# Moving the sweeps over the 8-bit weights, and their maximum over partitions, to earlier places of a fused transformer kernel

## What is computed

```
x = x + tanh(g_xattn[0]) * L0_xattn(layernorm(x), ctx, mask, mask, Wq, bq, Wk, bk, Wv, bv)   # 16 heads
x = x + tanh(g_ffn[0])   * L0_ffn(layernorm(x), w_gate, w_up, w_down)
x = x + tanh(g_xattn[1]) * L1_xattn(layernorm(x), k, fside, ctx, ctx, 8)                    # long convolution
x = x + tanh(g_ffn[1])   * L1_ffn(layernorm(x), w_fc, w_proj)

L0_ffn:  gate = sigmoid(bitlinear(x, w_gate)); up = bitlinear(x, w_up); bitlinear(gate * up, w_down)
         bitlinear: x per row rounded to 8 bits (scale max|x|/127), w rounded to {-1, 0, 1} * mean|w|
L1_ffn:  _fp8_matmul(relu(_fp8_matmul(x, w_fc))^2, w_proj)
         _fp8_matmul: w scaled by scale_w = max(max|w| / 448, 1e-6) and cast to e4m3; x likewise
```

## Time and profile before

| | |
|---|---|
| median of 3 runs | 1229.68 us (1228.73 to 1229.90) |
| profiled execution, its own time | 1229.71 us |
| its span in the trace | 1227.9 us |
| PE busy | 1065.7 us, 87% |
| DVE busy | 994.6 us, 81% |
| ACT busy | 702.7 us, 57% |
| GpSimd busy | 514.1 us, 42% |

### The profile page before, as it was taken

How to read it: one execution, slowest core, us unless ns; L and a number is a source line. 1 busy time by engine, 2 the same in 40 slices (tenths; PEclk the granted TensorE clock), 3 DMA queues, 4 the chain that set the end, 5 groups by cost and what they waited for, 6 DMA issues and landing times. The chain is left out here.

```text
span 1227.9 us, 13948 instructions
## 1 busy us (share of the span) xinstructions
PE 1065.7 (87%) x4729; PEld 420.3 (34%) x4802; DVE 994.6 (81%) x1522; ACT 702.7 (57%) x846; POOL 514.1 (42%) x403
## 2 busy tenths in 40 slices
PE   3889889999999999778999979999999996379686
PEld 2444212222222222134444444444444443134232
DVE  4368879999999997298999947887888887687897
ACT  2777768888888888846566760110000000885996
POOL 2666313543543553711010118888878880000111
PEclk9989889999999999999999998999999997599789
DMA  9899834644644642151111111212121110000011
GB/s 322 264 383 379 267 121 128 189 123 137 191 124 133 197 125 84 41 198 36 51 38 50 35 56 35 69 52 69 52 68 52 61 59 1 0 1 1 18 52 69
DMA packets 73703, 132.89 MB, mean 108 GB/s; under 512 B 18336, under 2 KB 37152, under 8 KB 73120
## 3 DMA queue, kind: packets, MB, share of 16 engines
q1 hardware_dynamic: 73632, 132.00, 32.9%
HBM read 107.58 MB, written 22.02 MB: 106 GB/s over the span
## 5 line engine op out<-in xcount | busy, mean ns | idle before, releaser
L921 DVE TENSOR_REDUCE mneg<-ps_m 128x1 f32<-128x512 f32 x512 | 326.3, 684 | 35.5 <-PE ps_m L833 31.9
L1527 PE MATMUL ps_y<-kv,toeplitz_sb 128*128 128x512 f32 x640 | 279.2, 595 | 8.4 <-POOL kv L1457 8.4
L773 ACT ACTIVATE probs<-ps_s 128x1024 f32<-128x1024 f32 x256 | 250.7, 1023 | 41.8 <-PE ps_s L866 41.8
L1527 PEld LDWEIGHTS ps_y<-kv,toeplitz_sb 128*128 128x128 f32 x640 | 120.9, 191 | 154.8 <-issue 154.8
L866 PE MATMUL ps_s<-qk_stack 128*128 128x512 bf16 x473 | 132.8, 387 | 26.9 <-ACT probs L773 17.5
L876 PE MATMUL ps_o<-probs,v_all 128*17 128x512 f32 x1024 | 135.6, 602 | 0.2 <-ACT probs L773 0.2
L1457 POOL TENSOR_TENSOR kv<-vT,ctxT_sb 128x2048 f32<-128x2048 f32 x32 | 118.9, 3717 | 35.4 <-PE ps_y L1527 28.5
L1112 PE MATMUL ps_g<-w,xT_f 128*128 128x512 bf16 x492 | 116.7, 382 | 13.4 <-DVE h_f L1294 8.5
L833 PE MATMUL ps_m<-qk_stack 64*128 64x512 bf16 x512 | 112.7, 394 | 14.3 <-DVE mneg L921 6.7
L1501 ACT ACTIVATE w_anchor<-w_f 128x512 f32<-128x512 f32 x32 | 20.0, 627 | 164.9 <-DMA w_f<-in_w 164.9
L1590 DVE TENSOR_TENSOR z<-ps_y,ctxT_sb 128x1024 f32<-128x1024 f32 x64 | 77.7, 1217 | 43.3 <-PE ps_y L1527 43.3
(11 more groups left out here) (167 smaller groups left out, 1616.2 us busy)
## 6 DMA issues: line engine op xcount, KB each, us to landing
qk_stack<-qk_parts SPq DMA_DIRECT2D x192, 128.0 KB, 3.0
w_sweep<-in_w SPq DMA_DIRECT2D x8, 1536.0 KB, 12.0
qk_parts<-qk_part SPq DMA_DIRECT2D x16, 768.0 KB, 9.1
w_sweep<-in_w SPq DMA_DIRECT2D x16, 768.0 KB, 5.4
w_sweep<-in_w SPq DMA_DIRECT2D x16, 512.0 KB, 3.7
toeplitz_sb<-in_toeplitz SPq DMA_DIRECT2D x32, 256.0 KB, 2.6
w_f<-in_w SPq DMA_DIRECT2D x32, 256.0 KB, 2.9
v_rows<-vp SPq DMA_DIRECT2D x8, 544.0 KB, 10.1
```

Source lines behind the costliest of these rows:

```text
L773: nc.scalar.activation(pr[:, k % 2, 2 * slot:2 * slot + 2, :], S[:, 2 * slot:2 * slot + 2, :], ACT.Exp).then_inc(exp_done, 1)
L921: nc.vector.tensor_reduce(mneg[:, h, tc, hd:hd + 1], M[:, bank_, :], AX.X, ALU.max, negate=True).then_inc(max_red, 1)
L1527: mm = nc.tensor.matmul(Y[:, q % 3, l2, :], T[:, g % 2, (lt - m) * P:(lt - m + 1) * P], kv[:, g % 2, m, :], start=(m == 0), stop=(m == lt))
```

## The change

It moves work between stages and shifts buffers; no arithmetic is added or taken away.

- SP issues the first two loads of sweeps in attention's unit 15, when the scores of unit 14 are done, ahead of that unit's denominators; loads 2 and 3 stand ahead of the loads of ctxT. For this `w8c` moves to 28 to 36 KB, and `gate` of the convolution to where it fits.
- DVE prepares rows 0 and 1 and does sweeps 0 and 1 before tile 0. Tile t then does sweep t + 1, for t from 1 to 14: sweep 15 stands in tile 14, and tile 15 has none.
- `invert` of unit 15 moves from behind the third chunk of tile 0 to behind its first; the statistics of rows 14 and 15 move from tiles 0 and 1 to tiles 1 and 2; ln_vector and ln_scalar of these rows move from tile 2 to tile 4.
- GpSimd's maximum over partitions moves to behind update(12).
- DVE's first write to `z` in the convolution waits until the last take_down is done, as the new layout needs.

```diff
@@ attention, sync
             if last:
+                load_sweeps(sp)
                 gather_den(u, h, b)
@@ feed-forward, sync
+    def load_sweep(sp, i):
+        if i >= 2:
+            sp.wait_ge(w8m_ready, i - 1)
+        sp.dma_start(w8c[:, i % 2], A["w8"][2 * i:2 * i + 2].rearrange("m p l -> p m l"))\
+            .then_inc(w8c_loaded[i % 2], 16)
+
+    def load_sweeps(sp):
+        sp.wait_ge(scores_done, 2 * STEPS * (ROWT - 1))
+        load_sweep(sp, 0)
+        load_sweep(sp, 1)
...
@@ feed-forward, scalar
-                if c == 2 and same(t, 2):
+                if c == 2 and t == 4:
                     ln_scalar(core, act, 2)
@@ feed-forward, vector
         def finish_attention(t):
-            if t == 0:
-                invert(dve, ROWT - 1, 1, B - 1)
+            if t == 1:
                 att_statistics(dve, ROWT - 2)
-            elif t == 1:
+            elif t == 2:
                 att_statistics(dve, ROWT - 1)
-            else:
+            elif t == 4:
                 ln_vector(core, dve, 2)
...
         prepare(0, 0, 0)
+        prepare(1, 1, 1)
+        sweep(0, 0)
+        sweep(1, 1)
...
-                if c == 0 and not last:
-                    if not first:
-                        dve.wait_ge(xt_done, t)
+                if c == 0 and first:
+                    invert(dve, ROWT - 1, 1, B - 1)
+                if c == 0 and not first and not last:
+                    dve.wait_ge(xt_done, t)
                     prepare(t + 1, 1 - par, t + 1)
-                if c == 2 and not first:
-                    sweep(t - 1, 1 - par)
+                if c == 2 and not first and not last:
+                    sweep(t + 1, 1 - par)
...
             if last:
                 quantise(t, par, t)
-                sweep(t, par)
                 statistics(dve, t - 1)
@@ feed-forward, gpsimd
         for t in range(ROWT - 1):
             update(pool, t)
+            if t == ROWT - 4:
+                largest_weight(pool)
@@ long convolution
-    def gpsimd(pool):
+    def largest_weight(pool):
         pool.wait_ge(w8_run, ROWT)
         nc.gpsimd.partition_all_reduce(w8s[:, MA, :], core.w8_max, P, bass.bass_isa.ReduceOp.max)\
             .then_inc(w8_all, 1)
+
+    def gpsimd(pool):
...
             weights(g)
+            if g == 0:
+                dve.wait_ge(d_taken, ROWT)
             weigh(g, 0)
```

More of the change, by code:

```diff
@@ L633, in load_next, with sync @@
             load_constants(core, sp, 1, 1)
-    def sync(sp):
+    def sync(sp, load_sweeps):
         def gather_den(u, h, b):
@@ L1030, in phase_bitlinear @@
     KB = 1024
-    xn, xq, xT, sg, h, hq, hT, ds, sc, w8m, w8c = overlay(
+    xn, xq, xT, sg, h, w8c, sc, w8m, hq, hT, ds = overlay(
         nc, "ffn", 0, ("xn_f", [P, 2, L], F32), ("xq_f", [P, 2, L], BF16), ("xT_f", [P, 2, LT, P], BF16),
-        ("sg_f", [P, 2, L], F32), ("h_f", [P, 2, FF], F32), ("hq_f", [P, 2, FF], BF16), ("hT_f", [P, 2, KT, P], BF16),
-        ("down_sums", [P, 1, L], F32), ("sc_f", [P, 2, 16], F32), ("w8_max_t", [P, 2, 2], F32),
-        ("w8_sweep1", [P, 2, 2, L], F32))
+        ("sg_f", [P, 2, L], F32), ("h_f", [P, 2, FF], F32), ("w8_sweep1", [P, 2, 2, L], F32),
+        ("sc_f", [P, 2, 16], F32), ("w8_max_t", [P, 2, 2], F32), ("hq_f", [P, 2, FF], BF16),
+        ("hT_f", [P, 2, KT, P], BF16), ("down_sums", [P, 1, L], F32))
     core.cT, = overlay(nc, "cT", 92 * KB, ("ctxT_sb", [P, LT, B, C], F32))
@@ L1052, in phase_bitlinear @@
     wd = core.w3[:, 2].rearrange("p a b -> p (a b)").rearrange("p (k o) -> p k o", k=KT)
-    def sync(sp):
[L1055 to L1063, removed]
+    def load_sweep(sp, i):
[7 more added lines that the diff above has]
+        load_sweep(sp, 1)
+    def sync(sp):
+        load_sweep(sp, 2)
+        load_sweep(sp, 3)
         sp.wait_ge(x_updated, ROWT)
@@ L1066, in sync @@
             sp.dma_start(core.cT[:, lt], A["ctxT"][lt * P:(lt + 1) * P]).then_inc(core.cT_loaded, 16)
-        for t in range(2, ROWT):
-            tile(t, t % 2, False, t == ROWT - 1)
+        for i in range(4, ROWT):
+            load_sweep(sp, i)
     def tensor(pe, turn_in):
@@ L1297, in tile @@
                     chunk_max(t, par, c - 1)
-                if c == 0 and not last:
-                    if not first:
-                        dve.wait_ge(xt_done, t)
+                if c == 0 and first:
+                    invert(dve, ROWT - 1, 1, B - 1)
+                if c == 0 and not first and not last:
+                    dve.wait_ge(xt_done, t)
                     prepare(t + 1, 1 - par, t + 1)
-                if c == 2 and not first:
-                    sweep(t - 1, 1 - par)
-                if c == 2 and t < 3:
+                if c == 2 and not first and not last:
+                    sweep(t + 1, 1 - par)
+                if c == 2:
                     finish_attention(t)
@@ L1330, in update, with gpsimd @@
         nc.gpsimd.tensor_tensor(xt, xt, ds[:], ALU.add).then_inc(xf_updated, 1)
-    def gpsimd(pool):
+    def gpsimd(pool, largest_weight):
         for t in range(ROWT - 1):
             update(pool, t)
+            if t == ROWT - 4:
+                largest_weight(pool)
     after = (shift_ready, xq_ready, hq_ready, h_ready, d_taken, xf_updated, w8_run, update, statistics)
-    return Phase(sync, gpsimd, scalar, tensor, vector), after
+    return Phase(sync, gpsimd, scalar, tensor, vector), load_sweeps, after
 def phase_longconv(core, ctx, A, before):
@@ L1629, in vector @@
         statistics(ROWT - 1)
-    return Phase(sync, gpsimd, scalar, tensor, vector), turn_in, normalise_ahead, place
+    return Phase(sync, gpsimd, scalar, tensor, vector), turn_in, normalise_ahead, place, largest_weight
 TWO20 = 2.0 ** 20
@@ L2007, in build @@
          vector_first) = first
-        bt, rest = phase_bitlinear(core, ctx, A, *tail)
-        cv, turn_in, normalise_ahead, place = phase_longconv(core, ctx, A, rest)
+        bt, load_sweeps, rest = phase_bitlinear(core, ctx, A, *tail)
+        cv, turn_in, normalise_ahead, place, largest_weight = phase_longconv(core, ctx, A, rest)
         with nc.Block() as block:
@@ L2014, in _ @@
                 pj.sync(sp, load_first, load_next)
-                at.sync(sp)
+                at.sync(sp, load_sweeps)
                 bt.sync(sp)
@@ L2022, in _ @@
                 at.gpsimd(pool)
-                bt.gpsimd(pool)
+                bt.gpsimd(pool, largest_weight)
                 cv.gpsimd(pool)
```

5 lines of the change are left out of this document (2 added, 3 removed).

## The result

| | before | after |
|---|---|---|
| median | 1229.79 us (4 executions, 1228.73 to 1232.18) | 1219.53 us (4, 1218.88 to 1221.34) |
| ratio after to before | | 0.9913, 95% interval 0.9899 to 0.9928 |
| profiled execution | 1229.71 us | 1219.38 us |
| its span | 1227.9 us | 1217.6 us |
| first convolution | 739.65 us | 731.52 us |

A second set of 6 executions gave 0.9927 (0.9911 to 0.9943). The change saves about 10 us, where 11.6 were forecast.

What follows compares the result with a forecast made beforehand. The convolution is PE-bound but waits 8.4 us for GpSimd's kv, held by two code switches. Seam 7.8, clock 1.7 and start 1.1 - 0.5 + 0.9 + 0.6 sum to 11.6: 1229.7 to 1218.1 us, range 1215.5 to 1222.5.

Steps and rivals of the forecast that it cites:

- The switches and the missing gap: End of feed-forward: GpSimd's two switches (5.57, 6.90 us) run before update(13), so kv runs inside down(15) and PE continues without gap.
- Clock 1.7: Start of the convolution: without PE's gap its clock does not fall, 1.7 us gained (bounds 0 and 1.8).
- Seam 7.8: End of feed-forward to first convolution: PE goes on at about 731.8 instead of 739.65, 7.8 us gained.
- now waits until 718.9, 0.9 later than before ... it slips by 0.5 us: End of feed-forward: DVE's row 13 statistics wait for late update(13), so round_h(15) and down(15) slip by 0.5 us.
- GpSimd comes back later than reckoned: Rival, end of feed-forward: update(14) goes before L1247, DVE and its chain wait 1.3 us; 1219.4 us, chance 0.13.
- +1.1 - 0.5 + 0.9 + 0.6 = 2.1: Start of feed-forward: 1.1 us from tile 0, 0.5 lost to roundings, 0.9 from tile 1, 0.6 net from tile 2.
- Tile 0 gave its term: Tile 0: PE's fourth chunk no longer waits for DVE's second product behind prepare(1), 1.1 us gained.
- the 0.6: Tile 2: with ln_vector moved and PE in time, less the statistics moving in, net 0.6 us gained (bounds 0.6 either way).
- The roundings' 0.5: Before tile 0: prepare(1) beside GpSimd's last three roundings makes PE start 0.5 us later (bounds 0.2 and 1.6).
- The term of 0.9 for tile 1: Tile 1: GpSimd's last normalise comes earlier and delays prepare(2) less, 0.9 us gained (bounds 0 and 1.9).
- ln moved: nothing: Tiles 2 and 4: ln_vector moves to tile 4 with all it costs, since DVE is as full there; nothing gained.
- roundings and DVE exclude each other: Rival, start of feed-forward: each rounding waits for a prepare(1) operation, PE starts 1.6 us later, not 0.5; 1219.2 us, chance 0.10.

## Why the prediction was right, and where its terms were not

The time was forecast as 1218.1 us and is 1219.5, inside the range, and the mechanism is the one forecast: GpSimd's switches held the first kv, and the maximum now runs them where the first kv does not wait. DVE does, and that was priced too low.

- **The switches and the missing gap: right.** all_reduce and both switches kept their lengths; kv waits for place 7; PE has no idle time before the convolution. The kernel with the maximum put back has the old time.
- **Clock 1.7: right.** The convolution's busy time went from 279.2 to 277.5 us, in every profile in which PE did not wait for kv.
- **Seam 7.8: mis-sized, measured 6.0, and 4.7 to 6.0 in the five profiles that end so.** The step "now waits until 718.9, 0.9 later than before ... it slips by 0.5 us" saw the wait and took it for the only price. round_h slipped by 1.6 us against tile 15 (14.78 us behind its start in before, 16.39 after): 1.05 for the later start of L1252, 0.95 for its meeting update(14), less 0.4 for which ACT itself had been busy. That meeting was my second rival, "GpSimd comes back later than reckoned", with a chance of 0.13; its 1219.4 us is nearer to what came out than the forecast. It is the rule here, not the exception: update(14) was on time, 14.0 us behind the start of tile 15, in all five profiles, and the late update(13) pushes quantise to just that place, so that one of L1250 to L1252 was drawn out in each (to 0.79 to 2.33 us). So round_h slipped by 1.1 us more than forecast. Another 0.9 us I had at nothing: PE's wait grew from 1.66 to 3.26 us, and the transposes and down(15) ran at the low clock. From round_h to the convolution it was 9.75 us (9.75 to 10.96 in the five), and 8.81 where the statistics were moved. The two are 0.2 us more than the shortfall of 1.8, since without any slip the seam would have gained that much more than I had summed (32.17 to 23.59).
- **The start, +1.1 - 0.5 + 0.9 + 0.6 = 2.1: right in sum for the two profiles (2.0 at the start of tile 5), by luck.** Tile 0 gave its term and 0.3 more: from PE's first load to tile 1 it is 11.16 us against 12.60. Tiles 2 and 4 together gave 0.4 of the 0.6. The roundings' 0.5 is there in seven profiles of eight, though not in this one. The term of 0.9 for tile 1 failed: the step "`invert` comes 5 us earlier ... 0.7 us less" moved GpSimd's operations out of prepare(2) and weighed quantise(0) as "may wait 0.3 us"; it lost 1.6. Over all profiles the new order is worth 0.5 us, which is inside the scatter.
- **ln moved: nothing. Right**, 4.80 against 4.75 us.
- **Rival "roundings and DVE exclude each other": false as stated.** It asked for 1.6 us; the roundings grew by 0.4 to 0.7, and DVE's operations beside them were drawn out to at most 0.96 us (0.43 to 0.54 alone), none to the 1.49 of a rounding. By the Trainium skill, page "SBUF — State Buffer", section "Who interferes with whom", VectorE's two-port operations and GpSimd exclude each other for a whole instruction; the traces agree for L1252 beside GpSimd's operations with two inputs (2.24 us instead of 1.29), and not for the roundings. L1250, an operation on one number per partition, was drawn out beside two-input operations as well, from 0.16 to 0.62 to 1.12 us.

## What to carry to other kernels

When a long operation is moved off the path, follow what is queued behind whoever waits for its engine's next result: a wait ahead of the critical operation costs more than its length, since it can push that operation into a collision and PE into a low clock, while one five times as long behind it costs nothing. Move the waiter as well. And the price of a collision seen in one profile is no property of an order of work: compare several executions before you credit its removal.

## What the runs showed of the hardware

GpSimd pays for the maximum over partitions in both directions: it stands idle 5.57 to 6.57 us ahead of it and 6.76 to 7.53 us behind it in all 12 profiles that have it, whether tiles run beside it or not. With a plain copy in its place the time ahead was 0.26 us, spent waiting for DVE.

PE's clock can differ after the same work. The kernel before without the maximum, and the changed one with later statistics and the old start, have the same operations and gaps on PE here. Timeline of PE and windows of the first:

```profile
722.39 1.80 PE L1438 MATMUL ps_turn<-ident_sb,vT 128*128 128x128 f32 x8 [1.66 <-ACT vT L1425]
723.98 1.91 PE L1085 MATMUL ps_ht<-ident,hq_f 128*128 128x128 bf16 x16
```
```profile
722.06:724.06 2.00, 1.67 (x9) 1.64 (x10) 0.00 (x0) 1.27 (x3) 0.00 (x0) 0.62 0.64 187
724.06:726.06 2.00, 1.83 (x17) 1.57 (x15) 0.00 (x0) 1.58 (x3) 0.98 (x1) 0.52 0.57 206
```

and of the second:

```profile
719.50 1.12 PE L1446 MATMUL ps_turn<-ident_sb,vT 128*128 128x128 f32 x8 [1.66 <-ACT vT L1433]
720.46 1.06 PE L1090 MATMUL ps_ht<-ident,hq_f 128*128 128x128 bf16 x16
```
```profile
719.17:721.17 2.00, 1.67 (x21) 1.62 (x22) 0.00 (x0) 1.68 (x5) 0.00 (x0) 1.00 0.51 174
721.17:723.17 2.00, 1.20 (x11) 0.58 (x8) 0.00 (x0) 1.92 (x3) 1.66 (x1) 1.00 0.61 227
```

After the wait of 1.66 us the granted clock of the next 2 us was 0.62 in one and 1.00 in the other, and the first convolution came 1.05 us later against tile 15. Of nine profiles with that wait one fell; after 3.26 to 3.71 us all five did. What decides between them these runs don't show.
